# Second-layer expert sums and output norms move from VectorE to GpSimd in a two-layer decoder kernel

## What is computed

```python
x = _layernorm(x + _L0_ffn_ref(x, ...))     # top 2 of 8 experts per token
x = _layernorm(x + _L1_attn_ref(x, ...))
x = _layernorm(x + _L1_xattn_ref(x, ctx_1024, ctx_1024, ...))   # 8 heads, exponential gates
x = _layernorm(x + _L1_ffn_ref(x, ...))     # 8 experts, gates of the pooled sequence
```

## Time and profile before

| | us |
|---|---|
| runs | 1011.18, 1017.53, 1008.25 |
| median | 1011.18 |
| the profiled execution | 1009.8 |
| its span in the profile | 1008.1 |
| DVE busy | 527.1 |
| POOL busy | 163.0 |

### The profile page before, as it was taken

The page is one execution under the profiler, slowest core; times in us unless marked ns, Lnnn a source line. Parts: engine busy times, 40 slices in busy tenths (PEclk is TensorE's granted clock), DMA queues, the critical chain, the costliest instruction groups (busy, mean ns, idle before and its releaser), DMA issues.

```text
span 1008.1 us, 13899 instructions
## 1 busy us (share of the span) xinstructions
PE 745.5 (74%) x4570; PEld 481.1 (48%) x4570; DVE 527.1 (52%) x1934; ACT 383.9 (38%) x888; POOL 163.0 (16%) x207
## 2 busy tenths in 40 slices
PE   5788796887865986985984972999357568667665
PEld 4445354453422662662662751778336336344342
DVE  4435245252625945945946821111245784876865
ACT  3514436144222542542540541333024354344543
POOL 9300000000111005005004004000331411311020
PEclk8889899898966997997995985999787889788887
DMA  7500000010024026026024001141110100200000
GB/s 213 181 1 21 2 21 0 10 42 0 11 48 105 1 49 100 11 47 98 12 44 55 2 1 61 27 108 44 48 40 2 46 7 13 52 11 12 0 12 10
DMA packets 49246, 39.49 MB, mean 39 GB/s; under 512 B 11235, under 2 KB 42659, under 8 KB 49189
## 3 DMA queue, kind: packets, MB, share of 16 engines
q1 hardware_dynamic: 47140, 34.62, 15.7%
q0 software_dynamic: 2048, 4.20, 1.5%
HBM read 27.20 MB, written 11.60 MB: 38 GB/s over the span
## 4 chain that ended last, share of the span: by engine, by line
PE 54%; DVE 23%; issue 8%; ACT 7%; DMA 5%; SPq 2%; POOL 1%; DVEq 0%; ACTq 0%; POOLq 0%
PE bank L1247 4%; PE bank L1236 4%; PE bank L1349 3%; DVE R L2182 3%; DMA q_stack<-parts_dram 3%; PE bank L1130 2%; PE bank L990 2%; PE bank L1133 2%; PE bank L1143 2%; PE bank L1132 2%; PE bank L922 2%; DVE bank L1900 2%; PE bank L1102 2%; PE bank L1013 2%; PE bank L1050 2%
## 5 line engine op out<-in xcount | busy, mean ns | idle before, releaser
L1900 DVE CUSTOM_DVE_ANT_0 bank<-bank,add_q 128x256 f32<-128x256 f32 x256 | 100.1, 456 | 34.7 <-PE bank L1102 21.6
L1558 ACT ACTIVATE pT<-bank 128x512 f32<-128x512 f32 x128 | 76.1, 597 | 75.7 <-PE bank L1133 73.4
L1102 PE MATMUL bank<-k_stack,q_stack 96*128 96x256 bf16 x256 | 51.7, 300 | 31.0 <-DMA q_stack<-parts_dram 24.2
L1349 PE MATMUL bank<-XT,kpad 128*128 128x256 f32 (+1 forms) x256 | 60.8, 368 | 15.9 <-DVE cT L2124 15.9
L1130 PE MATMUL bank<-q_stack,k_stack 96*128 96x256 bf16 x256 | 70.3, 275 | 1.8 <-DVE mx L1900 1.8
L1132 PE MATMUL bank<-add_k,ident_b 128*128 128x256 bf16 x256 | 70.6, 276 | 0.0
L1133 PE MATMUL bank<-neg_max,head_sel 96*128 96x256 bf16 x256 | 70.5, 275 | 0.0
L1349 PEld LDWEIGHTS bank<-XT,kpad 128*128 128x128 f32 x256 | 49.9, 217 | 26.1 <-DVE cT L2124 17.7
L2124 DVE TENSOR_TENSOR cT<-bank,decay 128x384 f32<-128x384 f32 x64 | 35.1, 554 | 48.5 <-POOL decay L872 28.3
L1583 ACT ACTIVATE he<-bank 128x324 f32<-128x324 f32 x64 | 28.2, 441 | 69.4 <-PE bank L1236 63.9
L872 POOL TENSOR_SCALAR_AFFINE_SELECT decay<-decay 128x256 f32<-128x256 f32 x64 | 27.2, 426 | 159.5 <-ACT decay L1652 159.5
(11 more groups left out here) (412 smaller groups left out, 1680.8 us busy)
## 6 DMA issues: line engine op xcount, KB each, us to landing
k_stack<-parts_dram SPq DMA_DIRECT2D x48, 64.0 KB
q_stack<-parts_dram SPq DMA_DIRECT2D x24, 128.0 KB, 8.1
expert_in<-no_rows SPq DMA_DIRECT2D x8, 324.0 KB, 4.0
rows<-expert_in SPq DMA_DIRECT2D x8, 324.0 KB
expert_out<-rows_y SPq DMA_DIRECT2D x8, 324.0 KB
moe_w<-in_L_ffn_w_dram SPq DMA_DIRECT2D x1, 2048.0 KB
parts_dram<-k_parts SPq DMA_DIRECT2D x4, 384.0 KB, 2.8
parts_dram<-q_parts SPq DMA_DIRECT2D x12, 128.0 KB, 1.7
```

The costliest lines, as they stand in the source:

```text
L1102: last = pe.matmul(q_bank(n)[:, c * S:(c + 1) * S], q_stack[:, h // 2, b * S + c * P:b * S + (c + 1) * P], k_stack[:, h // 2, h % 2, b * S ...
L1349: last = pe.matmul(c_bank(n)[:, lo:lo + width], kpad2[:, h, b * S + c * P:b * S + (c + 1) * P], XT[:, par, q0:q0 + width], start=True, sto ...
L1558: act.activation(pT[:, g % 2, j], k_bank(n)[:].rearrange("p (c q) -> p c q", c=QC), ACT.Exp).then_inc(exp_ready.sem, 1)
L1900: last = dve.tensor_tensor_reduce(sc, sc, add_q[:, b * QC + c, :], 1.0, 2.0 * NEG, ALU.add, ALU.max, mx[:, c, h:h + 1])
```

## The change

- `expert_sum(i)` is new on POOL for i = 1, 2, 3: four `tensor_scalar` per sequence multiply the gathered rows by their gates in place, and two `tensor_tensor` add them and `vT_all` into `mix_sum`. It starts when the norm after the self-attention of the step before is done (`norm_1.at(i - 1)`, all of it), since that is the last reader of `mix_sum`. DVE keeps the sums of step 0 and the statistics of all steps. The copy of the gates is gone.
- The last norm of steps 0 to 2 is made on POOL, one chunk each behind units 2, 4, 6 and 8 of `keep_past` of the next step. DVE keeps that of step 3, and waits for `norm_5` before it overwrites `R`.
- `spot_i` holds the row numbers of all steps; they are converted once, before the first gather.
- The gathers are issued one step earlier: `gather(1)` when DVE has read the rows of step 0, `gather(2)` behind `expert_sum(1)` and ahead of `keep_past(0)`, `gather(3)` behind `expert_sum(2)` in step 0's end.

```diff
@@ gpsimd @@
             def gather(i):
 
-                wait_apart(pool, passed, *spots_ready.at(i))
                 for b in range(NB):
                     for n in [j * NC + b * QC + c for j in range(2) for c in range(QC)]:
-                        pool.indirect_dma_start(pair_rows[:, n, :], None, expert_out, bass.IndirectOffsetOnAxis(spot_i[:, n:n + 1], 0)).then_inc(gathered[b].sem, 16)
+                        pool.indirect_dma_start(pair_rows[:, n, :], None, expert_out, bass.IndirectOffsetOnAxis(spot_i[:, i * PAIRS + n:i * PAIRS + n + 1], 0)).then_inc(gathered[b].sem, 16)
+
+            def expert_sum(i):
+
+                pool.wait_ge(*norm_1.at(i - 1))
+                for b in range(NB):
+                    wait_apart(pool, passed, *gathered[b].at(i))
+                    chain = Chain(pool, pool_sum, (i - 1) * NB + b)
+                    batch = slice(b * QC, (b + 1) * QC)
+                    for j in range(2):
+                        for c in range(b * QC, (b + 1) * QC):
+                            n = i * PAIRS + j * NC + c
+                            last = pool.tensor_scalar(pair_rows[:, j * NC + c, :], pair_rows[:, j * NC + c, :], gates_all[:, n:n + 1], None, ALU.mult)
+                    chain.link(last, passed)
+                    chain.link(pool.tensor_tensor(mix_sum[:, batch], pair_rows[:, batch], vT_all[:, i * T + b * S:i * T + (b + 1) * S].rearrange("p (c d) -> p c d", c=QC), ALU.add), passed)
+                    chain.close()
+                    last = pool.tensor_tensor(mix_sum[:, batch], mix_sum[:, batch], pair_rows[:, NC + b * QC:NC + (b + 1) * QC], ALU.add)
+                    last.then_inc(summed.sem, 1)
+                pool.wait_ge(*summed.at(i - 1))
+
+            def output(i, c):
+
+                if c == 0:
+                    wait_apart(pool, passed, *rstd_5.at(i))
+                    if i > 0:
+                        wait_apart(pool, passed, *out_saved.at(i - 1))
+                pool.tensor_scalar(Y[:, c, :], R[:, c, :], mv_2[:, c, 0:1], rstd_2[:, c:c + 1], ALU.subtract, ALU.mult).then_inc(norm_5.sem, 1)
...
+                    if i > 0 and n in (2, 4, 6, 8):
+                        output(i - 1, n // 2 - 1)
...
+            wait_apart(pool, passed, *spots_ready.at(0))
             gather(0)
             context_values(0)
-            pool.wait_ge(*norm_1.at(0, NC))
+            pool.wait_ge(*var_1.at(0, NB))
             gather(1)
+            expert_sum(1)
+            gather(2)
             for i in range(STEPS):
                 keep_past(i)
                 if i + 1 < STEPS:
                     context_values(i + 1)
                 if i + 2 < STEPS:
-                    pool.wait_ge(*norm_1.at(i + 1, NC))
-                    gather(i + 2)
+                    expert_sum(i + 2)
+                if i + 3 < STEPS:
+                    gather(i + 3)
@@ vector, first(i, 0) @@
-                    chain.link(dve.tensor_copy(pair_gate[:], gates_all[:, i * PAIRS:(i + 1) * PAIRS]))
...
+                        else:
+                            dve.wait_ge(*summed.at(i - 1, b + 1))
@@ vector, second @@
-                    if n == 2 and i > 0:
-                        output(i - 1)
...
+                if i > 0:
+                    dve.wait_ge(*norm_5.at(i - 1))
                 normaliser(0, 3)
```

More of the change, by code:

```diff
@@ L240, in decoder_kernel, with counted_on @@
         ctxT = sb("ctxT", [P, T], scope=stacks)
-        def counted_on(old, per):
-            return Signal(old.sem, per, primed=old.before(STEPS)[1])
+        def counted_on(old, per, extra=0):
+            return Signal(old.sem, per, primed=old.before(STEPS)[1], extra=extra)
         b_x_loaded = signal("b_x_loaded", 32)
@@ L385, in decoder_kernel @@
         dve_b = signal("dve_b", 32)
-        dve_c1 = counted_on(dve_a, 28)
+        dve_c1 = counted_on(dve_a, 19, extra=8)
         dve_c2 = counted_on(dve_b, 62)
@@ L390, in decoder_kernel @@
         pool_c = counted_on(pred_a, 1)
+        pool_sum = counted_on(x_plus, 2)
         scope_a = ExitStack()
@@ L2007, in first @@
                 if n == 0:
[L2008 removed]
                     for b in range(NB):
[L2010 removed]
+                        batch = range(b * QC, (b + 1) * QC)
                         marks = {}
[L2012 to L2020 removed]
+                        if i == 0:
+                            dve.wait_ge(*gathered[b].at(i))
+                            for j in range(2):
+                                for c in batch:
+                                    m = j * NC + c
+                                    if j > 0:
+                                        chain.wait(marks[c])
+                                    marks[c] = chain.mark(dve.scalar_tensor_tensor(mix_sum[:, c, :], pair_rows[:, m, :], gates_all[:, m:m + 1],
+                                                                                   mix_sum[:, c, :] if j > 0 else vT_all[:, c * P:(c + 1) * P], ALU.mult, ALU.add))
+                        else:
+                            dve.wait_ge(*summed.at(i - 1, b + 1))
+                        for c in batch:
+                            if i == 0:
+                                chain.wait(marks[c])
                             marks[c] = chain.mark(dve.bn_stats(bn[:, c, :], mix_sum[:, c, :]))
[L2022 removed]
+                        for c in batch:
                             wait_apart(dve, passed, *chain.links.at(chain.step, marks[c]))
@@ L2074, in first @@
                     chain.close()
-            def output(i):
-                dve.wait_ge(*rstd_5.at(i))
-                if i > 0:
-                    dve.wait_ge(*out_saved.at(i - 1))
-                for c in range(NC):
-                    dve.tensor_scalar(Y[:, c, :], R[:, c, :], mv_2[:, c, 0:1], rstd_2[:, c:c + 1], ALU.subtract, ALU.mult).then_inc(norm_5.sem, 1)
             def second(i, following):
@@ L2198, in _ @@
             experts()
-            spots(0)
+            dve.tensor_copy(spot_i[:], spots_all[:]).then_inc(spots_ready.sem, 1)
             chain = Chain(dve, dve_c1, 0)
@@ L2204, in _ @@
                 second(i, i + 1 < STEPS)
-            output(STEPS - 1)
+            dve.wait_ge(*rstd_5.at(STEPS - 1))
+            dve.wait_ge(*out_saved.at(STEPS - 2))
+            for c in range(NC):
+                dve.tensor_scalar(Y[:, c, :], R[:, c, :], mv_2[:, c, 0:1], rstd_2[:, c:c + 1], ALU.subtract, ALU.mult).then_inc(norm_5.sem, 1)
 _TRANSPOSED = {"L0_attn_" + n + "T": "L0_attn_" + n for n in ("wq", "wk", "wv", "wo", "lin1", "lin2", "w1", "w2", "mem")}
```

16 lines of the change are left out of this document (2 added, 14 removed).

## The result

The changed kernel takes 1017.93 us (median of 12 runs), the kernel before 1011.99 us in the 12 runs beside it: a ratio of 1.0061, interval 1.0036 to 1.0085. It is slower by 0.6%, some 6 us; that is 0.9 us above the forecast range and 8 above the forecast. The profiled execution took 1020.49 us, its span 1018.8.

The account below looks back on a forecast made before the run. At the second layer's step starts PE was taken to wait for DVE's weighted sums. Terms -4.6 - 1.0 - 0.2 + 1.6 + 3.8 = -0.4 us took the profiled 1009.8 to 1009.4; forecast 1010 us, range 1003 to 1017.

Parts of the forecast that it names:

- Steps 1 and 2, the sums leave DVE: Start of steps 1 and 2: sums and gate copy leave the path, 2.3 us each, 4.6 us less.
- rival (d): Steps 1 and 2: sums don't come off the path, ACT or PE comes last; +5, 1015 us; chance 0.06.
- The clock behind them: PE behind the sums in steps 1 and 2: granted clock drops less, 0.5 us each, 1.0 us less.
- Step 0: Start of step 0: POOL's sum and eight gathers delay the first select; unit 1's multiply 3.8 us later.
- Rival (b): POOL slow in its own right, so step 0 loses 8.5 us; +4.3, 1014 to 1015 us; chance 0.20.
- Company in steps 0 and 1: Ends of steps 0 and 1: POOL's sums slow DVE beside them, 0.8 us each, 1.6 us more.
- rival (a): Steps 0 and 1: DVE and POOL fully block each other on the shared port; +6, 1016 us; chance 0.15.
- The output norms: Last norms moved to POOL: worth nothing in steps 1 and 2, where PE comes last; 0.2 us less in step 3.
- one conversion, an earlier `gather(1)`, a later save: Single row-number conversion, gather(1) 2.5 us earlier, result save some 10 us later: each worth nothing.
- the 1.9 us between the multiplies: Sign of being right: DVE's next multiply 1.9 us behind the first in steps 1 and 2, instead of 4.2.
- the select straight behind a gather: Sign of being right: first select of step 0 near 767, straight behind a gather on POOL.
- steps 1 and 2 were shorter: Sign of being right: steps 1 and 2 shorter by about 2 us each.

Follow-up runs that it names:

- e3: Changed kernel with gathers back between steps and the last norm back on DVE, so the sums alone are moved; 0.9998 of the kernel before.
- e12: Sums on POOL in their own tile, in pieces between selects, gather(2) split, norms on DVE, unread matmuls: 20 before unit 12's decays, 22 at units 2 and 3; 0.9884 of before.
- e5: `e3` plus 20 matmuls nobody reads on PE ahead of unit 12's decays; 0.9954 of the kernel before.
- e10: Changed kernel plus 20 matmuls nobody reads on PE ahead of unit 12's decays; 1.0010 of the kernel before.
- e6: Kernel before plus 20 matmuls nobody reads on PE ahead of unit 12's decays; 0.9985 of the kernel before.
- e11: Changed kernel, early gathers kept, weighted sums of steps 1 to 3 left out (part of the computation missing); 0.9908 of the kernel before.
- e7: `e3` with the weighted sums of steps 1 to 3 left out (part of the computation missing); 0.9935 of the kernel before.
- e1: Changed kernel with the gathers back between steps, only expert_sum(1) ahead of step 0; 0.9998 of the kernel before.
- e2: Changed kernel with the last norm back on DVE, behind unit 2; 1.0060 of the kernel before.
- e4: Kernel before with only the output norms moved to POOL; 1.0026 of the kernel before.

## Why the prediction was wrong

The forecast was 1010 us, a sum of -0.4; the profiles show +6.8 in layer 2, the runs +0.6%. Term by term:

- **Steps 1 and 2, the sums leave DVE, -4.6.** Right: 4.18 and 4.39 from unit 0 to unit 1 became 1.87 and 1.87, which is -2.3 and -2.5. In this sense rival (d), that they don't come off the path, is out; it was right about what a step gains in the end, for another reason.
- **The clock behind them, -1.0.** This step failed, in its sign. It looked for the clock only at the spot where the sums had been, and assumed that less idle time there can only help. There the units 1 to 5 take 0.35 and 0.46 more, at a granted clock of 0.50 where they had 0.56 (step 1, windows above); at 1.00 they take 3.28 (`e3`, step 0) or 3.68 (`e12`). And units 11 to 15, where it did not look, cost +1.5 in each step. That makes +3.8 in all and not -1.0. That the second part is the clock's is shown by the filling (`e5`, `e10`) and its control, the same filling where nothing had fallen (`e6`). The bounds, 0 to -4, took in no loss at all, although the kernel before has the drop at one gap (0.64 from 827 on the earlier trace rows) and not at another (1.00 behind the 3.06 us at 850): a clock that falls in some places is a cost of either sign wherever work moves.
- **Step 0, +3.8.** The mechanism was right and the term too small. Start and units 0 to 1 together came to 8.43 - 2.61 = +5.8. The `tensor_scalar` 128x128 took 0.58 from start to start, not 0.35: the eight took 2.34 + 2.50 = 4.8, not 2.8. The `tensor_tensor` took 0.72 for 0.62, 0.4 more in all; the 0.8 put in for company was hardly needed. So the sum took 8.4 and not 6.9; its start, the gap behind it and the gathers (10.0 for 9.8) came some 0.7 later together. The value taken, 0.35, lay below even the quarter of the only row of the same operation, 0.39, and the measured 0.58 is half more than that quarter: the time did not fall in proportion to the elements. Rival (b), step 0 decides, was right in direction: it put the point from which that loss eats the gain at a sum of 7.3 us, and 8.4 is above it. (Its own 11.6 us left out the 0.8 for company that the 6.9 beside it holds.)
- **Company in steps 0 and 1, +0.8 each.** Nearly right in size: +0.8 and +0.4 from unit 15 to the next step. Of the two only the first is shown to be the sum's: without sums but in the same queue (`e11`) the stretches take 32.15 and 32.56, for 32.82 and 32.39. It is a price of place: with a late gather ahead of the sum it is +1.2 and +1.5 (`e3` against `e7`), with the sum in pieces between the selects nothing there. The 0.8 for the start of step 0 was put on POOL's sum, which lost only 0.16 (2.50 for 2.34). It is DVE that loses there, 1.4 in `e1`; in the changed kernel that isn't felt, as POOL is later than DVE.
- **Full blocking, rival (a).** The mechanism is shown in single meetings, its price was not. DVE's `tensor_tensor` went from 0.41 to 0.85 beside one of POOL's of 0.72, and its conversion of one input from 0.27 to 0.84. The Trainium skill, SBUF — State Buffer, on engine ports, has it that "the other fully blocks"; for the two instructions of two inputs the trace agrees to within 0.13 us. For one input the page's rule asks for "a 2-port perf mode", and no row shows whether the conversion ran in one. POOL pays too: 3.07 for 2.34 over four `tensor_scalar`. But the 4.4 us more that the rival worked out for steps 0 and 1 did not come: it took ten meetings of 0.3 us in each step, and the two ends of a step together grew by 1.2. Eight of a sum's twelve instructions are `tensor_scalar`, beside which DVE's scans lost 0.06 and 0.13.
- **The output norms, -0.2; one conversion, an earlier `gather(1)`, a later save, 0.** Right within what can be told (`e2`: 1.0060 for 1.0061), though a chunk took 0.79 to 0.81 and not 0.35.

The miss is 7.2 us, from -0.4 to +6.8: 2.0 at the start of step 0 with its units 0 to 1, 4.8 at the clock, -0.4 at the company, 0.5 at units 1 to 5 of step 0, 0.2 for the norms that gave nothing, -0.2 at the sums of steps 1 and 2, and 0.3 in small differences elsewhere. Two thirds of it is the clock in steps 1 and 2, and no rival had it with this sign.

Of what was to be seen, the 1.9 us between the multiplies came, the select straight behind a gather came too, but 773.2 - 753.2 = 20 us behind the start of the norm and not 767 - 749.2 = 17.8; steps 1 and 2 were shorter by 0.1 and 0.4 and not by 2.

What stays open: why the same idle 3.06 us of PE lower the clock in one kernel, or one step of it, and not in another. The runs show that filling this gap keeps the clock up wherever it had fallen, and that a change which leaves the idle time as it is (`e4`) can bring the drop. They don't show what decides, and with one profile of each kernel not how often a drop comes in other executions.

## What to carry to other kernels

Work that is moved to an idle engine has to fit, with all that is queued beside it, into the cover that the next user there has: add up every instruction ahead of that user, sum and gathers, against the path of the other engines (here 18 us against 12), and not against the engine's idle share. Then look at every place where the matrix engine idles for some us, also ones far from the change: when time is taken off a path, the clock behind a later gap can take it back, and matmuls without a use, put into the gap, are a cheap test of that and here a cure; where the engine has no gap they only hold it up (`e12`, step 0). And give moved work that disturbs the busier engine a buffer of its own, so that it can be cut up and put where that engine waits.

## What was not expected of the hardware

- POOL's `tensor_scalar` with a scalar for each partition, 128x128 f32, takes 0.58 us, and with two such scalars 0.79 to 0.81; `tensor_tensor` 128x256 takes 0.72, a `DMA_INDIRECT` holds POOL for 1.25 from start to start.
- A DVE instruction that comes just behind the start of a `tensor_tensor` of POOL is drawn out to 0.15 and 0.28 us behind its end (0.84 for 0.27, 0.85 for 0.41), also one with a single input, the bf16 conversion; four `tensor_scalar` of POOL are drawn out to 3.07 for 2.34 beside DVE's `tensor_tensor` of 512 elements.
- PE after 3.06 us of idling: 0.82 us for four matmuls in one kernel, 1.49 in another, with the granted clock at 1.00 and 0.54; 17 of 27 such gaps had the drop behind them, none of 15 that were filled down to 0.88 us.
